# Expert attention: V of the last tokens for four experts at once, weights-times-V over all 141 queries, and the tail copies moved between the maxima

## The reference, cut to what matters

```python
for e in range(4):                       # wq, wk, wv, wo: (4, 192, 192)
    q, k, v = (heads(x @ w[e].T) for w in (wq, wk, wv))   # 12 heads of 16 channels
    scores = einsum('bhqd,bhkd->bhqk', q, k) * 0.25
    scores = where(mask, scores, -1e30)  # query i sees keys i-63 .. i
    attn = softmax(scores)
    outs.append(einsum('bhqk,bhkd->bhqd', attn, v) @ wo[e].T)
fused = concatenate(outs, -1)
return silu(fused @ w_gate.T) * (fused @ w_up.T)
```

## Time and profile before

| | |
|---|---|
| time, median of 3 runs | 1284.58 us (1283.99 to 1287.29) |
| the profiled execution's own time | 1284.13 us |
| its span | 1282.4 us |
| mean granted clock of TensorE | 0.921 |
| PE busy | 1166.7 us, 91% |
| DVE busy | 718.3 us, 56% |
| ACT busy | 764.9 us, 60% |
| POOL busy | 390.7 us, 30% |

### The profile page before, as it was taken

One profiled execution on the slowest core, in us unless ns is written; L12 is line 12 of the kernel. 1 busy time (PEld: TensorE's weight loads), 2 busy tenths in 40 slices (PEclk: granted clock), 3 DMA queues, 4 the chain that ended last, 5 costly groups with the idle time before them and its releaser, 6 DMA issues. The chain is left out here.

```text
span 1282.4 us, 33640 instructions
## 1 busy us (share of the span) xinstructions
PE 1166.7 (91%) x13103; PEld 929.7 (73%) x13103; DVE 718.3 (56%) x2290; ACT 764.9 (60%) x3342; POOL 390.7 (30%) x529
## 2 busy tenths in 40 slices
PE   6789986899998599985899999999999999996898
PEld 4479964777775265324899999999999999983466
DVE  7344455666675303324677677667766776766201
ACT  1154524777773725413887778778877887783421
POOL 1100012333332154302434443444344434441000
PEclk9779975999998599966999999999999999996799
DMA  7000000000002600001000000000000000000000
GB/s 241 24 1 1 1 1 1 2 2 2 2 1 54 139 1 1 1 1 44 2 3 2 2 2 3 3 2 3 3 3 2 2 3 3 3 2 1 0 29 28
DMA packets 34733, 19.83 MB, mean 15 GB/s; under 512 B 24592, under 2 KB 32016, under 8 KB 34576
## 3 DMA queue, kind: packets, MB, share of 16 engines
q1 hardware_dynamic: 34432, 17.20, 5.0%
q10 hardware_dynamic: 144, 0.49, 0.1%
HBM read 15.12 MB, written 1.77 MB: 13 GB/s over the span
## 5 line engine op out<-in xcount | busy, mean ns | idle before, releaser
L1860 POOL TENSOR_TENSOR e_W<-e_W,e_RS 128x384 f32<-128x384 f32 x256 | 204.1, 829 | 331.1 <-DVE e_RS L1789 331.1
L1732 ACT ACTIVATE e_W<-banks,e_MX 128x128 f32<-128x128 f32 x768 | 269.5, 390 | 14.7 <-DVE e_MX L1777 10.9
L1732 ACT ACTIVATION_READ_ACCUMULATOR e_W<-banks,e_MX 128x1 f32 x768 | 175.9, 229 | 0.0
L1588 PE MATMUL banks<-XT,e_wqk 128*128 128x141 f32 x768 | 111.8, 296 | 13.8 <-DVE e_GU L1831 8.4
L1726 ACT COPY e_PT<-banks 128x512 f32<-128x512 f32 x128 | 70.2, 587 | 83.7 <-PE banks L1636 83.6
L1636 PE MATMUL banks<-ident,e_W 128*128 128x128 f32 x768 | 108.8, 277 | 1.8 <-POOL e_W L1860 1.3
L1588 PEld LDWEIGHTS banks<-XT,e_wqk 128*128 128x128 f32 x768 | 98.1, 193 | 16.2 <-issue 11.6
L1600 PE MATMUL banks<-e_wv,XT 128*128 128x192 f32 (+1 forms) x512 | 95.1, 329 | 0.2 <-ACT e_K L1721 0.2
L1117 POOL TENSOR_TENSOR f_W<-f_W,f_RS 128x423 f32<-128x423 f32 x64 | 56.4, 893 | 117.1 <-DVE f_RST L1101 109.1
L469 POOL TENSOR_TENSOR rstd<-veps,nhalf 128x6 f32<-128x6 f32 x15 | 20.6, 1375 | 233.3 <-DVE veps L435 233.3
L1636 PEld LDWEIGHTS banks<-ident,e_W 128*128 128x128 f32 x768 | 87.5, 144 | 5.7 <-DVE e_ON L1814 1.8
(11 more groups left out here) (252 smaller groups left out, 2656.4 us busy)
## 6 DMA issues: line engine op xcount, KB each, us to landing
xp<-in_patches_dram SPq DMA_DIRECT2D x4, 768.0 KB, 8.6
H<-in_h_dram SPq DMA_DIRECT2D x1, 1728.0 KB, 10.7
out_dram<-H SPq DMA_DIRECT2D x6, 288.0 KB, 2.3
e_g<-in_e_gu_dram SPq DMA_DIRECT2D x1, 1536.0 KB, 8.0
e_o<-in_e_o_dram SPq DMA_DIRECT2D x4, 192.0 KB, 5.6
e_wqk<-in_e_qk_dram SPq DMA_DIRECT2D x8, 96.0 KB, 2.5
e_wqk<-in_e_qk_dram SPq DMA_DIRECT2D x24, 32.0 KB, 2.3
e_wv<-in_e_v_dram SPq DMA_DIRECT2D x4, 192.0 KB, 2.6
```

The lines of the kernel that those rows point to most:

```text
L1588: mm = nc.tensor.matmul(bank[6][:, m * SEQ:(m + 1) * SEQ], w[:, c, m * P:(m + 1) * P], XT[:, c, t0:t0 + SEQ], start=(m == 0 and c == 0), s ...
L1732: ex = nc.scalar.activation(W[n % 2][:, t, :], bank[i][:, x * P:(x + 1) * P], ACT.Exp, bias=MX[:, t:t + 1], accum_out=SM[n % 2][:, t:t + 1])
L1860: nc.gpsimd.tensor_tensor(x, x, RS[n % 2][:, 3 * i:3 * i + 3].unsqueeze(2).broadcast_to([P, 3, P]), ALU.mult).then_inc(s_nm, 1)
```

## The change

- **V.** `project_v` multiplies 128 tokens for each expert. The 13 last tokens are done once per sample, when n % 4 is 0, for its four experts: expert e in column strip e, so that V of these 13 tokens stands at partitions 32e to 32e+12 of bank 6 and is copied by one instruction to `VT`. The second segment no longer overlaps the first: keys are 0 to 127 and 128 to 140.
- **Weights.** `WT` is widened to all 141 keys; keys 0 to 64 of the tail queries are zeros, set once. The tail's transposition becomes four instructions: 128 keys of 104 and of 52 rows, and 13 keys of 104 and of 52 rows.
- **Copies of the tail's weights.** Three on DVE instead of one: two into the last 13 columns of `PT` (now 141 wide), one into `PTT` at partitions 32e to 32e+12.
- **attend.** The first pass has 141 columns. The second pass adds for the 13 tail queries the 13 last keys, in row strip e and four column strips. Heads 8 to 11 now come out in bank 4 instead of in bank 5.
- **Order and waits.** The maxima are split: the weights copy and the tail copies of n-1 stand between the first and the last maxima of n. The ON copy of heads 8 to 11 comes first, and the first transposition group (bank 4) now waits for it.
- **Set-up.** Two more memsets for `WT`; those of V are four of 128x384 instead of two of 128x768.

```diff
 W = [psb(f"e_W{i}", [P, 12, P]) for i in range(2)]
-WT = [psb(f"e_WT{i}", [P, 2, NKT]) for i in range(2)]
+WT = [psb(f"e_WT{i}", [P, 2, SEQ]) for i in range(2)]
 SM, RS = ([psb(f"e_{x}{i}", [P, 12]) for i in range(2)] for x in ("SM", "RS"))
 SMT, RST = ([psb(f"e_{x}{i}", [P, 2]) for i in range(2)] for x in ("SMT", "RST"))
-PT = psb("e_PT", [P, 12, P])
-PTT = psb("e_PTT", [NKT, 12, NT])
-VP = [psb(f"e_V{i}", [P, 2, 12, HP]) for i in range(2)]
+PT = psb("e_PT", [P, 12, SEQ])
+PTT = psb("e_PTT", [P, 12, NT])
+VP = [psb(f"e_V{i}", [P, 12, HP]) for i in range(2)]
+VT = [psb(f"e_VT{i}", [P, 12, HP]) for i in range(2)]
 ON = psb("e_ON", [P, 2, SEQ])
...
 S0 = 3 * P
-SEGS = ((0, P), (KT, NKT))
-O0 = 2 * NTR
+TAIL_ROWS = (NTR, 4 * NT)
+TR0, O0 = 12 * NT, 24 * NT
 slot_of = {h: t for t, h in enumerate(SLOT_HEADS)}
...
 
+def v_ready(n):
+    return n + 1 + n // EXPERTS + 1
+
 def tail_rows(buf):
...
             elif n > 1:
-                pe.wait_ge(s_v, 2 * n - 2)
+                pe.wait_ge(s_v, v_ready(n - 2))
             w, t0 = ew[n % EXPERTS][0], tokens(n)
...
             pe.wait_ge(s_q, 5 * last)
-            w, t0 = ew[n % EXPERTS][1], tokens(n)
-            for i, (k0, nk) in enumerate(SEGS):
+            t0 = tokens(n)
+            for c in range(2):
+                mm = nc.tensor.matmul(bank[6][:, 0:C], XT[:, c, t0:t0 + P], ew[n % EXPERTS][1][:, c, :],
+                                      start=(c == 0), stop=(c == 1), skip_group_check=True)
+            if n % EXPERTS == 0:
                 for c in range(2):
-                    mm = nc.tensor.matmul(bank[6][0:nk, i * C:(i + 1) * C], XT[:, c, t0 + k0:t0 + k0 + nk],
-                                          w[:, c, :], start=(i == 0 and c == 0), stop=(c == 1),
-                                          skip_group_check=True)
+                    for e in range(EXPERTS):
+                        mm = nc.tensor.matmul(bank[6][HP * e:HP * e + NT, C:2 * C], XT[:, c, t0 + P:t0 + SEQ],
+                                              ew[e][1][:, c, :], start=False, stop=(c == 1),
+                                              tile_position=(0, HP * e), skip_group_check=True)
             mm.then_inc(s_vp, 1)
...
         def transpose_tail(n):
-            nc.tensor.transpose(bank[5][0:NKT, 0:NTR], WT[n % 2][0:NTR, 0, :], ident[0:NTR, 0:NTR])
-            nc.tensor.transpose(bank[5][0:NKT, NTR:2 * NTR], WT[n % 2][0:NTR, 1, :],
-                                ident[0:NTR, 0:NTR]).then_inc(s_tr, 1)
+            for lo, k0, nk in ((0, 0, P), (TR0, P, NT)):
+                for i, rows_i in enumerate(TAIL_ROWS):
+                    tr = nc.tensor.transpose(bank[5][0:nk, lo + i * NTR:lo + i * NTR + rows_i],
+                                             WT[n % 2][0:rows_i, i, k0:k0 + nk], ident[0:rows_i, 0:rows_i])
+            tr.then_inc(s_tr, 1)
 
         def attend(n):
-            pe.wait_ge(s_pd, 2 * n + 2)
-            pe.wait_ge(s_v, 2 * n + 2)
-            strip1 = 2 * (n % 2)
-            seen = set()
-            for heads in ((0, 2, 4, 6), (1, 3, 5, 7), (8, 10), (9, 11)):
-                for h in heads:
-                    c, col = (h // 2, O0) if h < 8 else (strip1 + (h - 8) // 2, O0 + SEQ)
-                    nc.tensor.matmul(bank[5][HP * c:HP * (c + 1), col:col + P], VP[n % 2][:, 0, h, :],
-                                     PT[:, slot_of[h], :], start=(c not in seen), stop=(h % 2 == 1),
+            pe.wait_ge(s_pd, 4 * n + 4)
+            pe.wait_ge(s_v, v_ready(n))
+            e, strip1 = n % EXPERTS, 2 * (n % 2)
+            groups = ((5, O0, ((0, 0), (2, 1), (4, 2), (6, 3))), (5, O0, ((1, 0), (3, 1), (5, 2), (7, 3))),
+                      (4, 0, ((8, strip1), (10, strip1 + 1))), (4, 0, ((9, strip1), (11, strip1 + 1))))
+            for b, col, heads in groups:
+                for h, c in heads:
+                    nc.tensor.matmul(bank[b][HP * c:HP * (c + 1), col:col + SEQ], VP[n % 2][:, h, :],
+                                     PT[:, slot_of[h], :], start=(h % 2 == 0), stop=False,
                                      tile_position=(0, HP * c), skip_group_check=True)
-                    seen.add(c)
-            for heads in ((0, 2, 4, 6), (1, 3, 5, 7), (8, 10), (9, 11)):
-                for h in heads:
-                    c, col = (h // 2, O0) if h < 8 else (strip1 + (h - 8) // 2, O0 + SEQ)
-                    mm = nc.tensor.matmul(bank[5][HP * c:HP * (c + 1), col + P:col + SEQ],
-                                          VP[n % 2][0:NKT, 1, h, :], PTT[:, h, :], start=False,
-                                          stop=(h % 2 == 1), tile_position=(0, HP * c),
+            lo = HP * e
+            for b, col, heads in groups:
+                for h, c in heads:
+                    mm = nc.tensor.matmul(bank[b][HP * c:HP * (c + 1), col + P:col + SEQ],
+                                          VT[n // EXPERTS % 2][lo:lo + NT, h, :], PTT[lo:lo + NT, h, :],
+                                          start=False, stop=(h % 2 == 1), tile_position=(lo, HP * c),
                                           skip_group_check=True)
...
         pe.wait_ge(s_mk, MASKS_BUILT)
-        pe.wait_ge(s_set, 5)
+        pe.wait_ge(s_set, 7)
         project_qk(0)
...
                 if n >= 2:
-                    pe.wait_ge(s_pd, 2 * n - 3)
+                    pe.wait_ge(s_o, 2 * n - 3)
                 pe.wait_ge(s_nm, 5 * n - 3)
...
             act.wait_ge(s_tr, 4 * n + u + 1)
-            nc.scalar.copy(PT[:, 4 * u:4 * u + 4, :], bank[4 + u][:, 0:4 * P]).then_inc(s_pa, 1)
+            nc.scalar.copy(PT[:, 4 * u:4 * u + 4, 0:P], bank[4 + u][:, 0:4 * P].rearrange("p (x q) -> p x q", x=4)
+                           ).then_inc(s_pa, 1)
 
...
 
-        def maxima(n):
+        def first_maxima(n):
             dve.wait_ge(s_sc, n + 1)
...
                                         negate=True).then_inc(s_mx, 1)
+
+        def last_maxima(n):
             dve.wait_ge(s_st, n + 1)
...
             dve.wait_ge(s_tr, 4 * n + 3)
-            nc.vector.tensor_copy(PT[:, 8:12, :], bank[4][:, 0:4 * P]).then_inc(s_pd, 1)
+            nc.vector.tensor_copy(PT[:, 8:12, 0:P], bank[4][:, 0:4 * P].rearrange("p (x q) -> p x q", x=4)
+                                  ).then_inc(s_pd, 1)
 
...
             dve.wait_ge(s_tr, 4 * n + 4)
-            nc.vector.tensor_copy(PTT[:, :, :], bank[5][0:NKT, 0:12 * NT]).then_inc(s_pd, 1)
+            slots = PT[:, :, P:SEQ].rearrange("p (i x) q -> p i x q", x=3)
+            nc.vector.tensor_copy(slots[:, :, 0:2, :],
+                                  bank[5][:, 0:NTR].rearrange("p (i x q) -> p i x q", x=2, q=NT)
+                                  ).then_inc(s_pd, 1)
+            nc.vector.tensor_copy(slots[:, :, 2, :].rearrange("p (a b) q -> p b a q", b=2),
+                                  bank[5][:, NTR:TR0].rearrange("p (b a q) -> p b a q", a=2, q=NT)
+                                  ).then_inc(s_pd, 1)
+            lo = HP * (n % EXPERTS)
+            nc.vector.tensor_copy(PTT[lo:lo + NT, :, :], bank[5][0:NT, TR0:O0]).then_inc(s_pd, 1)
 
...
             dve.wait_ge(s_vp, n + 1)
-            for i, (k0, nk) in enumerate(SEGS):
+            for i, to in enumerate((VP[n % 2], VT[n // EXPERTS % 2])[:2 if n % EXPERTS == 0 else 1]):
                 nc.vector.tensor_copy(
-                    VP[n % 2][0:nk, i, :, :].rearrange("p (g a) x -> p g (a x)", a=2)
+                    to[:, :, :].rearrange("p (g a) x -> p g (a x)", a=2)
                     .rearrange("p g (b d) -> p g b d", d=HD)[:, :, 0:4:3, :],
-                    bank[6][0:nk, i * C:(i + 1) * C].rearrange("p (g b d) -> p g b d", b=2, d=HD)
+                    bank[6][:, i * C:(i + 1) * C].rearrange("p (g b d) -> p g b d", b=2, d=HD)
                 ).then_inc(s_v, 1)
...
                 dve.wait_ge(s_gu, n)
+            lo = n % 2 * C1
+            nc.vector.tensor_copy(ON[lo:lo + C1, 1, :], bank[4][lo:lo + C1, 0:SEQ]).then_inc(s_o, 1)
             nc.vector.tensor_copy(ON[:, 0, :], bank[5][:, O0:O0 + SEQ]).then_inc(s_o, 1)
-            lo = n % 2 * C1
-            nc.vector.tensor_copy(ON[lo:lo + C1, 1, :], bank[5][lo:lo + C1, O0 + SEQ:O0 + 2 * SEQ]
-                                  ).then_inc(s_o, 1)
 
...
         for i in range(2):
-            nc.vector.memset(VP[i][:, :, :, :], 0.0)
+            nc.vector.memset(WT[i][:, :, :], 0.0).then_inc(s_set, 1)
+        for to in VP + VT:
+            nc.vector.memset(to[:, :, :], 0.0)
         nc.vector.memset(GU[:, :, :].rearrange("p b (s t) -> p b s t", t=SLOT)[:, :, :, SEQ:SLOT], 0.0
                          ).then_inc(s_set, 1)
-        dve.wait_ge(s_set, 5)
+        dve.wait_ge(s_set, 7)
         evacuate_q(0)
...
             if n < N:
-                maxima(n)
+                first_maxima(n)
             if 1 <= n <= N:
...
             if n < N:
+                last_maxima(n)
                 reciprocals(n, 0, 6, 2)
```

(4 more changed lines are left out.)

## The result

| | before | changed |
|---|---|---|
| median | 1284.36 us (4 runs) | 1341.56 us (4 runs) |
| profiled execution: span | 1282.4 us | 1339.9 us |
| granted clock, mean | 0.921 | 0.910 |

The ratio is 1.0439, with a 95% interval of 1.042 to 1.0457: slower by 57 us. The prediction said 1328, within 1308 to 1343, and slower. The mean period is 9.21 us where it forecast 9.23; its total was 13.6 us short, for two reasons outside the periods, the ends of the stage and the stages ahead of it. One of the runs of the kernel before that were taken for comparison with the experiments was slow (1881.39 us at a granted clock of 0.55) and stands in no ratio.

What follows compares the result with a forecast made beforehand. After the change the loop through four engines, not PE, was to bound every period: 62 x 9.23 = 572.3, less 529.9 = +42.4, plus 1.6 for the stage's ends = +44.0 us, giving 1328 us; range 1308 to 1343.

Steps and rivals of the forecast that it cites:

- the ends of the stage: Start and end of the expert attention: +0.7 us for memsets, +0.9 in the last iteration, together +1.6.
- The loop: Four engines, from PE's transpositions through maxima, exponentials and ON copies back to PE: 8.25 us before, 9.23 after.
- The period is the loop's in all of them: Every kind of iteration: loop of 8.99 to 9.47 us lies above PE's work, at most 8.76.
- PE's work: PE's own time per iteration: mean of four 8.18 to 8.43 us, against 8.48 before.
- busy about 90%: PE in the expert attention after the change, with gaps of 0.5 to 1.5 us and the clock unchanged.
- The price of jumps: DVE instructions in the loop starting at another partition begin about 0.12 us later: mean 0.24 us an iteration.
- Rival 1: The loop without the price of jumps: 8.99 us a period, 1313 us (1308 to 1317); chance 0.15.
- the gain, and small: PE's mean work per iteration falls to 8.18 to 8.43 us from 8.48.
- Rival 2: PE's saving counts and the loop stays hidden, if under 8.4 us: mean period 8.44, 1279 us, faster; chance 0.09.
- Rival 3: Second pass of attend in one row strip doesn't overlap: 2.88 us instead of 0.53, 1417 us; chance 0.04.
- The start of the sum: Kernel before: short period 8.25 us equals the loop's sum; PE's work 8.87 in long iterations, 8.08 in short ones.
- The upper ends of the terms: PE's tiling changes cost time: up to 0.17 us before the second pass, 0.34 for two around V of the tail.

Runs made afterwards that it cites:

- old order: Changed kernel, but DVE does both last maxima right behind the first ones, weights copy and tail copies after them: 1317.99 us, ratio 1.0258.
- ON copies early: Both ON copies moved on DVE between the second and third group of reciprocals: changed kernel 1311.62 us; same edit on the kernel before 1281.17 us.
- strip 0: Changed kernel, but the 13 last keys' weights always go to partitions 0 to 12 and are multiplied in row strip 0: 1324.65 us, ratio 1.03.
- equal rows: Changed kernel with ON copies early, plus the tail's transpositions of four heads done over all 104 rows instead of 52: 1305.98 us, ratio 1.0157.
- the second profile of the changed kernel: Changed kernel measured and profiled once more, nothing edited: 1335.49 us, ratio 1.038.

## Why the prediction was right, and what was off

- **The loop** was right in mechanism, place and size. Foretold 9.23 in the mean; for experts 1 and 2, where it alone sets the period, 9.35 and 9.2, measured 9.31 and 9.18. Undone in three ways (old order, ON copies early, strip 0) the mean period fell each time to what was worked out, within 0.03 us; made alone on the kernel before, the new order lengthened the short periods alone. The 61 periods together make 40.4 of the 57 us.
- **"The period is the loop's in all of them"** was wrong, and here luck helped. For experts 0 and 3 the loop was foretold at 9.0 and 9.35 and PE's work turned out at 9.04 and 9.31, level with it. Had PE's work grown by a little more, the mean of 9.23 would have been too low. With the loop cut (ON copies early) the mean is still 8.92: of the 0.66 us a period, 0.29 come back with the loop and 0.37 stay as PE's longer work. So PE, foretold to be "busy about 90%", is busy 98%.
- **The price of jumps** (the choice between 8.99 and 9.23) was right: 0.11 us each at partition 32 too. Rival 1 is out by the run in strip 0. The Trainium skill's rule in "VectorE: DVE Perf Modes", section "Two Vector instructions with no wait between them", agrees: a jump of one quadrant holds as one of two does.
- **PE's work** was wrong. "8.42 to 8.59 us in long iterations" is 9.04; "8.25 to 8.76" with V of the tail is 9.31; "7.63 to 7.80" is 8.35 with the ON copies early. The failing terms: tail transpositions +0.10, measured +0.61; first pass and change of tiling +0.07 to 0.24, measured +0.40; V of the tail 0.62 to 0.96, measured 1.0. The second pass was cheaper than foretold, 0.35 instead of 0.53. I had priced transpositions by their columns. So "the gain, and small" was a loss of 0.2 in long and short iterations and of more with V of the tail: 8.92 in the mean, against 8.51 for the kernel before with the same edit. Rival 2 would not have come out faster even if its condition held. Rival 3 is out too: the second pass takes 0.35 us, not 2.88.
- **The start of the sum** had a misread row: the period from 812.05 ends at 820.21, not at 820.30, and is 8.16 us. That is PE's own work in a short iteration, as the ON copies early on the kernel before confirm; 8.08 was too low. The sum of 8.25 for the loop stands, since the periods between tail maxima are 8.87 and 8.25 in turn; but it was 0.09 above PE's work and not 0.17:

```profile
820.21 1.00 PEld L1636 LDWEIGHTS banks<-ident,e_W 128*128 128x128 f32 x8
```

- **Drains.** The upper ends of the terms were nearer than the lower ones, and still too low: 0.22 us before the second pass, 0.23 and 0.32 around V of the tail, 0.29 between the transpositions of 104 and of 52 rows (0.11 with equal rows). The Trainium skill, "TensorEngine Tiling (Array Packing)", section Key Properties, says that a change of tiling mode drains TensorE. These waits agree with it.
- **The ends of the stage**: "+1.6" was too small. In the second profile of the changed kernel, whose earlier stages took as long as before, the span is 51.6 us longer: 0.8 ahead of the stage, 2.3 more to the tail maxima of iteration 1, 40.3 in the 61 periods, 3.8 in the last one (12.05 instead of 8.25) and 4.4 after it. In the prediction's own terms, 62 periods of 9.21, the ends cost 9.6 us. Most of that came with PE's wait of 2.47 us and the half clock behind it, which I had not looked for: in strip 0 alone, where the clock stayed full, the last period and the time after it are only 0.8 and 0.6 us longer than before, and the ends cost 2.9 in all. The argument that gaps of 0.5 to 1.5 us leave the clock alone held inside the stage (granted clock 1.00 from 640 to 1130 us), but at its end the gap is longer.
- **Outside**: about 6 us of the first measurement are not the change's.

## What to carry to other kernels

When one engine is 99% busy, still look whether the periods are alike. Here two lengths differed by 0.62 us where the work that tells them apart takes 0.71 (8.87 less 8.16): a second limit, a loop through other engines, lay beside the first, and what was put into that loop counted. When two limits are that close, work out both after the change; one of them coming out right does not prove the other. An instruction that waits for a far engine should not stand, on its in-order queue, ahead of one that a busy engine needs; moving the two ON copies ahead of it took 24 to 30 us from the changed kernel, and made the kernel before faster by 0.26%. Splitting small matmuls and transpositions into other shapes can cost several times what their columns say: look in the trace for the waits between shapes. Only one such wait, 0.18 us at the change from 104 to 52 rows, was taken away here by giving both the same rows, and most of it came back as longer passes.

## What the runs showed of the hardware

- Four transpositions of 104x128, 52x128, 104x13 and 52x13 took 0.82 us, two of 104x76 0.21 us.
- 24 loads and matmuls of 13x32 by 13 columns in one row strip and four column strips took 0.35 us, 15 ns each, faster than the 22 ns of those with 76 rows.
- PE after a wait of 2.47 to 2.48 us had its half clock in both profiles of the changed kernel (eight transpositions in 1.57 us), after one of 2.22 us in strip 0 alone its full clock (0.86 us). The single wait does not decide it: in the kernel before with the new order alone, PE had only four transpositions (0.42 us) between a pause of 0.57 and one of 1.33 us at the end of the stage, and the clock fell within the four transpositions behind them (0.62 us instead of 0.42).
- A DVE copy or maximum whose partitions start 32 further on or back than those of the instruction before it began 0.11 us later.
